# Mamba block: decay exponents by broadcast rows and a relu on ScalarE in place of matmuls with masked row constants

## The chip, the cores and the metric

The kernel runs on one core of a Trainium2 chip. The metric is the device time of one execution in microseconds (us); lower is better. TensorE is PE here, VectorE is DVE, ScalarE is ACT, GpSimd is POOL, and the queue of SyncE, which issues the DMAs, is SP.

## The reference

A block on 1024 tokens of width 512: a layer norm, then x plus a Mamba-2 mixer plus a small mixture of LoRA experts. The mixer is what matters. It has 128 heads of 64 channels, 8 groups of a 128-wide state, and chunks of 128 tokens:

```python
A_cum = jnp.cumsum(A_dt, axis=-1)                      # per head, inside a chunk
L = jnp.exp(_segsum(A_dt))                             # exp(A_cum[l]-A_cum[s]) for s<=l, else 0
Y_diag = jnp.einsum('bzlhn,bzshn,bhzls,bzshp->bzlhp', Cc, Bc, L, xch)
decay_states = jnp.exp(A_cum[..., -1:] - A_cum)
states = jnp.einsum('bzlhn,bhzl,bzlhp->bzhpn', Bc, decay_states, xch)
...
Y_off = jnp.einsum('bzlhn,bzhpn,bhzl->bzlhp', Cc, prev, jnp.exp(A_cum))
Y = (Y_diag + Y_off).reshape(b, s, H, P) + hs * D[None, None, :, None]
g = y * jax.nn.silu(gate)                              # then a group norm and out_proj
```

## The kernel before

The heads are worked in 16 stages s of 8 heads, and each stage in 8 chunks c of 128 tokens, so the main loop has 128 slots, m = 8s + c. Each engine runs its own list of instructions in order, and semaphores join them. Ahead of the loop stand the norm, the router, the LoRA part, the step sizes and their running sum A_cum (in the tile Q[1]).

In slot m, PE works through this, each item into one or two of the eight PSUM banks:
- T(m+1): four transposes of the 512 head channels of the next chunk (L285), and D(m+1): four bf16 matmuls (L292) that build, for all 8 heads, the 128x128 exponents A_cum[l] - A_cum[s], with about -3e38 where s > l. Their operands are constants (identity and mask, 64 rows) and rows of A_cum split into three bf16 parts, which three small DMAs per slot bring (`sp_rows`, tiles RM and RL). D takes banks 2 and 3.
- BG(m+1), in even stages alone: the transpose of B and the product G = B C of the chunk (L298, L299).
- A: input projection of a later stage, 12 matmuls for half a tile of 1024 tokens. Even stages have one half in each slot, odd stages 2, 1, 1, 2, 2, 1, 1, 2 halves, the last stage none.
- Off(m), St(m), Y(m): the old state's share, the new state, and the chunk's own share (32 small matmuls, L406, from EM and xch).
- O(m-1), 12 matmuls; GTr(m), transposes of the gated yb (L421); GT(m+1), 12 matmuls for the gate.

ACT in slot m (`act_front` first): the copy hsr of T(m+1) (L462); in even stages the copies BH, Gt and CH; the exponential over D(m+1) in PSUM (L476), ahead of which it loads its table; then tap (L446), SH, DH, the square sq of yb (L604), pl in even stages, gTh, OH at c=0, AH, the silu of a finished tile (L450), and the silu of GT(m+1) (L624).

DVE in slot m (`dve_front`, `dve_decay`): xch and dxh of the next chunk from T(m+1), with a wait for hsr; BL; then yb <- Off(m) (L807), the state S (L817), the product EM(m+1) = exp(D) * Gt (L659), yb <- Y(m) (L829), yb times the gate (L832), which releases sq on ACT and GTr(m) on PE; then the convolution of a tile (L635, three passes), gTl, and at c=0 OL. POOL makes dhs = hsr * D (L883), adds it to yb between L807 and L829 (L914), and makes the low parts SL, DL, CL, AL and GL.

A bank is given out again when the readers of its last user are through (`freed`). T's bank is free after xch and dxh, and in even stages St(m) takes the bank of T(m+1).

Of the kernel before, what the change touches and what calls it, by code (L numbers as in the profile page):

```python
# [6 lines left out]
def mamba_moe_block_kernel(nc, x, wa, wg, wo, wdt, cw, cbias, nw, dtb, alog, dvec, wbase, wrt, wla, wlb,  # L7
                           ident_c, rm_c, rl_c, ex_c, out):
# [3 lines left out]
    T, NS, NC, NB = 1024, 16, 8, 8  # L12
# [5 lines left out]
    par_d = nc.dram_tensor("par_d", [NS, 3, 8, NC, 128], bf16, kind="Internal").ap()  # L18
    sct_d = nc.dram_tensor("sct_d", [NC, 128, NS, 3, 8], f32, kind="Internal").ap()
# [33 lines left out]
    jobs += [("A", 3, (2, 3)), ("A", 4, (0, 1)), ("A", 5, (2, 3)), ("T", 0, (5,)), ("BG", 0, (6,)), ("D", 0, (2, 3)), ("GT", 0, (4,))]  # L53
# [43 lines left out]
    with ctx:  # L97
# [3 lines left out]
        def sem(name):  # L101
# [30 lines left out]
        dhs = sb("dhs", [128, 512])  # L132
# [10 lines left out]
        ident = sb("ident", [128, 128])  # L143
        Dbc = sb("Dbc", [128, 128])
# [53 lines left out]
        s_t, s_hsr, s_d, s_exp, s_bg, s_gb, s_bh, s_ch, s_bl, s_cl = (  # L198
            sem(n) for n in ("tp_", "hsr_", "dp", "exp", "bgp", "gb", "bh_", "ch_", "bl_", "cl_"))
# [15 lines left out]
            "T": lambda m: [(s_xch, m + 1)] + ([(s_dxh, n7(m))] if m % 8 != 7 else []),  # L215
            "D": lambda m: [(s_m, m + 1)], "BG": lambda m: [(s_bl, ngc(m))], "GT": lambda m: [(s_g, m + 1)],
# [33 lines left out]
        xs = [pl[0], pl[1], al[0], al[1], Sa, hsr, dxh, yb]  # L250
        sct_b = (xch[0], dhs, EM[1][:, 0:512], EM[1][:, 512:1024], S, pl[0], pl[1], al[0])
# [27 lines left out]
        def pe_front(m):  # L279
# [30 lines left out]
        def pe_program():  # L310
# [71 lines left out]
            for m in range(M + 1):  # L382
# [3 lines left out]
                if m < M:  # L386
# [16 lines left out]
                    for h in range(8):  # L403
                        at_ = (h % 2) * 512 + (h // 2) * 128
# [52 lines left out]
        def act_front(m):  # L457
            s, c = divmod(m, 8)
            se.wait_ge(s_t, m + 1)
            if m:  # L460
                se.wait_ge(s_dhs, m)
            se.activation(hsr[:, :], bank("T", m), ACT.Copy).then_inc(s_hsr, 1)  # L462
            if s % 2 == 0:
                o = bank("BG", m)
                se.wait_ge(s_bg, ngc(m))
                if s:
                    if c != 7:
                        se.wait_ge(s_stp, n7(m - 8))
                    if c:
                        se.wait_ge(s_off, n0(m - 8))  # L470
                    se.wait_ge(s_m, m - 7)
                se.activation(BH[:, c, :], o[:, 0:128], ACT.Copy).then_inc(s_bh, 1)
                se.activation(Gt[:, c, :], o[:, 128:256], ACT.Copy).then_inc(s_gb, 1)
                se.activation(CH[:, tok(c)], Cx[:, tok(c)], ACT.Copy).then_inc(s_ch, 1)
            se.wait_ge(s_d, m + 1)
            se.activation(pair("D", m), pair("D", m), ACT.Exp).then_inc(s_exp, 1)  # L476
# [15 lines left out]
        def act_program():  # L492
# [36 lines left out]
            se.wait_ge(s_rowsc, 4)  # L529
# [576 lines left out]
```

## Time and profile before

| | us |
|---|---|
| median of 3 runs | 1811.13 (1809.97 to 1813.1) |
| the profiled execution | 1813.75 |
| its span, first to last instruction | 1812.4 |
| PE busy | 1733.1 |
| ACT busy | 1279.0 |
| DVE busy | 1226.1 |
| POOL busy | 952.7 |
| mean granted TensorE clock | 0.992 of full |

The share of busy time is over the whole span. What sets the time of a slot is read from the engines' timelines: who waited for whom, and how long before it was needed each result was there. An "E slot" below is a slot of an even stage, an "O slot" one of an odd stage. The stretch from 776 to 988 us is one pair of stages (6 and 7), and E slots start again behind it. Start times of such slots are about 12.55 us apart for E slots.

### The profile page before, as it was taken

The page shows a single profiled execution, that of the slowest core. Times are in us where ns is not written, and L with a number is a line of the kernel's source. Part 1 is how long each engine was busy: PE and PEld are TensorE (multiplying, and loading weights), DVE is VectorE, ACT ScalarE, POOL GpSimd, SP SyncE. Part 2 cuts the span into 40 slices and gives each one's busy share as a digit, 9 for nine tenths or more (in the row PEclk, how much of TensorE's full clock was granted, in tenths as well). Part 3 has the DMA queues.
Part 4 walks back from the last instruction along what each step waited for, and adds up shares of the span by engine and source line. Part 5 has one row for each costly group of instructions (what it writes and reads, how often), then busy time and mean ns, then how long its engine had stood idle before and what let it go on. Part 6 is the DMA issues. An engine that isn't in the chain of part 4 may idle for free.

```text
span 1812.4 us, 32217 instructions
## 1 busy us (share of the span) xinstructions
PE 1733.1 (96%) x11748; PEld 1398.0 (77%) x11748; DVE 1226.1 (68%) x1594; ACT 1279.0 (71%) x1920; POOL 952.7 (53%) x973
## 2 busy tenths in 40 slices
PE   5989999999999999999999999999999999999988
PEld 3667878777887878778787777878787787877776
DVE  5846667766767658775677657776577656767666
ACT  4348776677767777777766777677776777667775
POOL 2125555545655555465555546555465555655475
PEclk8899999999999999999999999999999999999999
DMA  3141032220322113221332113231132212221022
GB/s 124 53 138 52 25 103 90 78 63 32 118 87 93 37 54 104 90 75 38 101 92 78 63 32 116 77 101 34 46 118 78 87 38 93 88 85 51 26 95 83
DMA packets 90699, 137.46 MB, mean 76 GB/s; under 512 B 38922, under 2 KB 40338, under 8 KB 86320
## 3 DMA queue, kind: packets, MB, share of 16 engines
q1 hardware_dynamic: 90544, 135.40, 23.7%
q8 instruction: 96, 1.57, 0.4%
q14 instruction: 59, 0.48, 0.1%
HBM read 97.34 MB, written 38.01 MB: 75 GB/s over the span
## 4 chain that ended last, share of the span: by engine, by line
PE 77%; DVE 10%; POOL 5%; issue 3%; ACT 2%; DMA 1%; SPq 1%; DVEq 0%; ACTq 0%; POOLq 0%
PE P L239 22%; PE P L241 20%; PE P L240 20%; PE P L406 5%; DVE hsX L635 4%; POOL GL L867 4%; PE P L285 3%; PE P L292 3%; PE P L421 2%; DMA EM<-in_rl_c 1%; DVE OL L853 1%; POOL yb L914 1%; ACT hsX L450 1%; DVE yb L829 1%; DVE yb L832 1%
## 5 line engine op out<-in xcount | busy, mean ns | idle before, releaser
L914 POOL TENSOR_TENSOR yb<-yb,dhs 128x512 f32<-128x512 f32 x112 | 143.8, 1284 | 634.3 <-DVE yb L807 634.3
L239 PE MATMUL P<-xh,AH 128*128 128x512 f32 x656 | 268.4, 409 | 1.1 <-POOL AL L862 1.1
L635 DVE SCALAR_TENSOR_TENSOR hsX<-P,cwt,hsX 128x1023 f32<-128x1023 f32 (+2 forms) x192 | 245.6, 1279 | 19.2 <-ACT hsX L446 14.6
L241 PE MATMUL P<-xh,AL 128*128 128x512 f32 x656 | 256.8, 391 | 0.0
L240 PE MATMUL P<-xl,AH 128*128 128x512 f32 x656 | 256.6, 391 | 0.0
L239 PE MATMUL P<-GH,xh 128*128 128x512 f32 x544 | 233.1, 429 | 8.1 <-POOL GL L867 7.3
L807 DVE TENSOR_TENSOR yb<-P,SC 128x512 f32<-128x512 f32 x112 | 77.3, 690 | 221.3 <-PE P L241 221.3
L645 DVE TENSOR_TENSOR xch<-P,SC 128x512 f32<-128x512 f32 x128 | 88.0, 687 | 190.0 <-ACT hsr L462 189.8
L241 PE MATMUL P<-GH,xl 128*128 128x512 f32 x544 | 216.0, 397 | 0.0
L239 PE MATMUL P<-OH,gTh 128*128 128x512 f32 x512 | 213.1, 416 | 2.5 <-issue 1.8
L240 PE MATMUL P<-GL,xh 128*128 128x512 f32 x544 | 214.6, 394 | 0.0
L604 ACT ACTIVATE sq<-yb 128x512 bf16<-128x512 f32 x128 | 80.9, 632 | 181.7 <-DVE yb L832 181.7
L241 PE MATMUL P<-OH,gTl 128*128 128x512 f32 x512 | 201.2, 393 | 0.0
L240 PE MATMUL P<-OL,gTh 128*128 128x512 f32 x512 | 200.5, 392 | 0.0
L873 POOL TENSOR_TENSOR SL<-S,SH 128x512 fp32r<-128x512 f32 x112 | 145.2, 1296 | 69.8 <-ACT SH L484 65.2
L406 PEld LDWEIGHTS P<-xch,EM 128*64 128x64 f32 x4096 | 129.9, 138 | 50.0 <-issue 42.8
L476 ACT ACT_TABLE_LOAD x128 | 164.2, 1283 | 2.2
L862 POOL TENSOR_TENSOR AL<-AR,AH 128x512 fp32r<-128x512 f32 x82 | 107.5, 1311 | 110.9 <-ACT AH L435 110.9
L659 DVE TENSOR_TENSOR EM<-P,Gt 128x1024 f32<-128x1024 f32 x128 | 155.5, 1215 | 3.5 <-ACT P L476 3.5
L406 PE MATMUL P<-xch,EM 128*64 128x64 f32 x4096 | 147.5, 225 | 4.5 <-DVE xch L645 3.3
L876 POOL TENSOR_TENSOR DL<-dxh,DH 128x512 fp32r<-128x512 f32 x112 | 145.1, 1296 | 9.6 <-ACT DH L490 9.6
L241 PEld LDWEIGHTS P<-xh,AL 128*128 128x128 f32 x656 | 123.7, 189 | 26.8
(188 smaller groups left out, 4031.9 us busy)
## 6 DMA issues: line engine op xcount, KB each, us to landing
AR<-in_wa SPq DMA_DIRECT2D x80, 256.0 KB, 2.9
TS<-in_wg SPq DMA_DIRECT2D x16, 1024.0 KB, 5.7
TS<-in_wo SPq DMA_DIRECT2D x16, 1024.0 KB, 5.4
part_d<-pl SPq DMA_DIRECT2D x64, 256.0 KB, 2.9
pl<-part_d SPq DMA_DIRECT2D x64, 256.0 KB, 2.7
al<-acc_d SPq DMA_DIRECT2D x64, 256.0 KB, 3.0
acc_d<-al SPq DMA_DIRECT2D x58, 256.0 KB, 3.0
RL<-par_d SPq DMA_DIRECT2D x256, 6.0 KB
```

What stands on the lines that cost most here:

```text
L239: te.matmul(o, ah_, bh_, start=(first and i == 0), stop=False)
L240: te.matmul(o, ah_, bl_, start=False, stop=False)
L241: r = te.matmul(o, al_, bh_, start=False, stop=(last and i == n - 1))
L406: r = te.matmul(o[f:f + 64, h * 64:(h + 1) * 64], EM[m % 2][:, at_ + f:at_ + f + 64], xch[m % 2][:, h * 64:(h + 1) * 64], start=True, stop ...
L476: se.activation(pair("D", m), pair("D", m), ACT.Exp).then_inc(s_exp, 1)
L635: ve.scalar_tensor_tensor(out=o[:, d:T], in0=raw[:, 0:T - d], scalar=cwt[:, n, 3 - d:4 - d], in1=o[:, d:T], op0=ALU.mult, op1=ALU.add).the ...
L645: ve.tensor_tensor(h8(xch[m % 2][:, :]), h8(o), bc(SC[s % 2][:, c, 0, :]), ALU.mult).then_inc(s_xch, 1)
L659: ve.tensor_tensor(EM[m % 2][:, :].rearrange("p (h l) -> p h l", h=8), pair("D", m).rearrange("p (h l) -> p h l", h=8), Gt[:, c, :].unsque ...
L862: pe_.tensor_tensor(AL[i % 2][:, :, :], AR[i % 2][:, :, :], as_f(AH[i % 2][:, :, :]), ALU.subtract).then_inc(ring_lo, 1)
L873: pe_.tensor_tensor(SL[:, :], S[:, :], as_f(SH[:, :]), ALU.subtract).then_inc(s_sl, 1)
L876: pe_.tensor_tensor(DL[:, :], dxh[:, :], as_f(DH[:, :]), ALU.subtract).then_inc(s_dl, 1)
L914: pe_.tensor_tensor(yb[:, :], yb[:, :], dhs[:, :], ALU.add).then_inc(s_tp, 1)
```

## The change

1. D(m) is no longer made by PE. A_cum goes to DRAM in f32 (`acr_d`), and one DMA per slot broadcasts the 8 rows of 128 values to all 128 partitions (tile AB, 512 KB written). ACT then makes the exponents in banks 2 and 3, head by head, with eight relus of 128x128: relu(A_cum[s] - A_cum[l]), where A_cum[s] is a per-partition bias from a fourth row group in SC. One exponential with scale -1 follows. Entries with s > l are 1 instead of 0.
2. G is masked once with a triangle by DVE when it leaves PSUM; ACT's copy Gt is gone.
3. hsr is gone. DVE makes dhs = T * D itself from PSUM (two buffers), behind dxh. POOL's product is gone. T's bank is free after dhs.
4. Ahead of the loop, the two loads of row constants, four casts of them and the split of A_cum into bf16 parts (five DVE operations, three stores) are gone; there are eight stores of A_cum, one more constant load, and SC is a third larger.

```diff
@@ pe_front
-            banks_free("D", m)
-            te.wait_ge(rows_in[m % 2], 48 * (m // 2 + 1))
-            v = pair("D", m).rearrange("p (q h l) -> p q h l", q=2, h=4)
-            for q in range(2):
-                for f in range(2):
-                    r = te.matmul(v[:, q, :, f * 64:(f + 1) * 64], RL[m % 2][0:79, q, f, :],
-                                  RM[m % 2][0:79, q::2, f * 64:(f + 1) * 64], start=True, stop=True)
-            r.then_inc(s_d, 1)
@@ act_front
-            se.activation(hsr[:, :], bank("T", m), ACT.Copy).then_inc(s_hsr, 1)
...
-                se.activation(Gt[:, c, :], o[:, 128:256], ACT.Copy).then_inc(s_gb, 1)
...
-            se.wait_ge(s_d, m + 1)
-            se.activation(pair("D", m), pair("D", m), ACT.Exp).then_inc(s_exp, 1)
+            for h in range(8):
+                r = se.activation(E[:, h, :], AB[m % 2][:, h, :], ACT.Relu, bias=SC[s % 2][:, c, 3, h:h + 1], scale=-1.0)
+            r.then_inc(s_gap, 1)
+            se.wait_ge(s_gap, m + 1)
+            se.activation(E[:, :, :], E[:, :, :], ACT.Exp, scale=-1.0).then_inc(s_exp, 1)
@@ dve_front
-            ve.wait_ge(s_hsr, m + 1)
+            ve.wait_ge(s_t, m + 1)
...
+            if m > 1:
+                ve.wait_ge(s_tp, n0(m - 2))
+                ve.wait_ge(s_t2, m - 1)
+            ve.tensor_tensor(h8(dhs[m % 2][:, :]), h8(o), bc(Dbc[:, 8 * s:8 * s + 8]), ALU.mult).then_inc(s_dhs, 1)
...
+                ve.tensor_tensor(Gt[:, c, :], o[:, 128:256], tri[:, :], ALU.mult).then_inc(s_gb, 1)
@@ pool_front
-            pe_.tensor_tensor(h8(dhs[:, :]), h8(hsr[:, :]), bc(Dbc[:, 8 * s:8 * s + 8]), ALU.mult).then_inc(s_dhs, 1)
@@ sp_rows
-                sp.wait_ge(s_d, m - 1)
-            sp.dma_start(RM[r][64:67, :, :], par_d[s, :, :, c, :]).then_inc(rows_in[r], 16)
-            for f in range(2):
-                sp.dma_start(RL[r][67:79, :, f, :],
-                             par_d[s, :, :, c, :].rearrange("i (h q) l -> (i h) q l", q=2)).then_inc(rows_in[r], 16)
+                sp.wait_ge(s_gap, m - 1)
+            sp.dma_start(AB[m % 2][:, :, :], acr_d[s, c:c + 1].broadcast_to([128, 8, 128])).then_inc(rows_in[m % 2], 16)
@@ dve_program, ahead of the loop
-            ve.wait_ge(rc_in, 32)
-            for r in range(2):
-                ve.tensor_copy(RM[r][0:79, :, :].rearrange("p h l -> p (h l)"), Qe[0:79, :]).then_inc(s_rowsc, 1)
-                ve.tensor_copy(RL[r][0:79, :, :, :].rearrange("p a b c -> p (a b c)"), EM[0][0:79, 0:512]).then_inc(s_rowsc, 1)
```

The order of ACT in an E slot of the first stage, from the silu of the gate to the square. Before (waits in brackets, by semaphore):

```order
L624 ACTIVATE P<-P 128x512 [waits gtp]
L462 ACTIVATE hsr<-P 128x512 [waits dhs_,tp_]
L472 ACTIVATE BH<-P 128x128 [waits bgp]
L473 ACTIVATE Gt<-P 128x128
L474 ACTIVATE CH<-Cx 128x128
L476 ACT_TABLE_LOAD
L476 ACTIVATE P<-P 128x1024 [waits dp]
L484 ACTIVATE SH<-S 128x512 [waits sl_,offp,st_]
L490 ACTIVATE DH<-dxh 128x512 [waits dl_,stp,dxh_]
L604 ACTIVATE sq,sqs<-yb 128x512 [waits sq_,g_]
```

The same place after the change:

```order
L613 ACTIVATE P<-P 128x512 [waits gtp]
L456 ACTIVATE BH<-P 128x128 [waits bgp]
L457 ACTIVATE CH<-Cx 128x128
L465 ACTIVATE P<-AB,SC 128x128 [waits m_,sc_in0,rows_in0]
L465 ACTIVATE P<-AB,SC 128x128 x7
L468 ACT_TABLE_LOAD
L468 ACTIVATE P<-P 128x1024 [waits gap]
L476 ACTIVATE SH<-S 128x512 [waits sl_,offp,st_]
L482 ACTIVATE DH<-dxh 128x512 [waits dl_,stp,dxh_]
L593 ACTIVATE sq,sqs<-yb 128x512 [waits sq_,g_]
```

Two copies have gone and eight relus stand ahead of the table load; the number of table loads is the same.

The order of DVE in an E slot, from gTl of one slot to yb of the next. Before:

```order
L848 TENSOR_TENSOR gTl<-P,gTh 128x512 [waits gth]
L645 TENSOR_TENSOR xch<-P,SC 128x512 [waits yp,sc_in0,hsr_]
L649 TENSOR_TENSOR dxh<-P,SC 128x512 [waits dl_]
L652 TENSOR_TENSOR BL<-P,BH 128x128 [waits gb]
L807 TENSOR_TENSOR yb<-P,SC 128x512 [waits sq_,gtr,offp]
L817 TENSOR_TENSOR S<-P,Sa 128x512 [waits sl_,sa_,stp]
L659 TENSOR_TENSOR EM<-P,Gt 128x1024 [waits exp,gb]
L829 TENSOR_TENSOR yb<-P,yb 128x512 [waits tpl,yp]
L832 TENSOR_TENSOR yb<-P,yb 128x512 [waits sg_,t2]
```

The same place after the change:

```order
L836 TENSOR_TENSOR gTl<-P,gTh 128x512 [waits gth]
L634 TENSOR_TENSOR xch<-P,SC 128x512 [waits yp,sc_in0,tp_]
L638 TENSOR_TENSOR dxh<-P,SC 128x512 [waits dl_]
L642 TENSOR_TENSOR dhs<-P,Dbc 128x512 [waits t2,tpl]
L648 TENSOR_TENSOR BL<-P,BH 128x128 [waits bh_]
L651 TENSOR_TENSOR Gt<-P,tri 128x128
L795 TENSOR_TENSOR yb<-P,SC 128x512 [waits sq_,gtr,offp]
L805 TENSOR_TENSOR S<-P,Sa 128x512 [waits sl_,sa_,stp]
L659 TENSOR_TENSOR EM<-P,Gt 128x1024 [waits yp,exp,gb]
L817 TENSOR_TENSOR yb<-P,yb 128x512 [waits tpl,yp]
L820 TENSOR_TENSOR yb<-P,yb 128x512 [waits sg_,t2]
```

dhs and Gt have joined the part between gTl and yb, and xch waits for the transposes themselves (tp_) and no longer for ACT's copy (hsr_).

## Rows read from the trace of the kernel before

**Rows 1.** The page, parts 1 and 4: busy time by engine; the chain that ended last.
```profile
PE 1733.1 (96%) x11748; PEld 1398.0 (77%) x11748; DVE 1226.1 (68%) x1594; ACT 1279.0 (71%) x1920; POOL 952.7 (53%) x973
...
PE 77%; DVE 10%; POOL 5%; issue 3%; ACT 2%; DMA 1%; SPq 1%; DVEq 0%; ACTq 0%; POOLq 0%
```

**Rows 2.** Timeline of PE in an E slot: start us, us, engine, line, out<-in.
```profile
803.22 0.60 PE L292 MATMUL P<-RM,RL 79*128 79x256 bf16 x4
803.66 0.27 PE L298 MATMUL P<-ident,Bx 128*128 128x128 f32 x1
...
824.67 0.60 PE L421 MATMUL P<-ident,yb 128*128 128x128 f32 x4
```

**Rows 3.** Groups by line and shape, ACT: busy us, mean ns, idle before.
```profile
L614 ACT ACTIVATE gTh<-P 128x512 fp32r<-128x512 f32 x128 | 76.2, 596 | 29.7 <-PE P L421 28.6
...
L618 ACT ACTIVATE OH<-TS,nwt 128x512 fp32r<-128x512 f32 x64 | 40.9, 715 | 1.8 <-DMA TS<-in_wo 1.8
...
L472 ACT ACTIVATE BH<-P 128x128 fp32r<-128x128 f32 x64 | 17.3, 270 | 5.0 <-PE P L299 2.1
```

**Rows 4.** Timeline of ACT: four scaled copies in a row.
```profile
891.35 2.56 ACT L618 ACTIVATE OH<-TS,nwt 128x512 fp32r<-128x512 f32 x4
```

**Rows 5.** Timeline of ACT: the exponentials of five slots, and one hsr copy.
```profile
806.15 1.01 ACT L476 ACTIVATE P<-P 128x1024 f32<-128x1024 f32 x1
...
819.19 1.01 ACT L476 ACTIVATE P<-P 128x1024 f32<-128x1024 f32 x1
...
883.34 0.60 ACT L462 ACTIVATE hsr<-P 128x512 f32<-128x512 f32 x1 [0.42 <-POOL dhs L883]
...
885.25 1.01 ACT L476 ACTIVATE P<-P 128x1024 f32<-128x1024 f32 x1
...
897.62 1.01 ACT L476 ACTIVATE P<-P 128x1024 f32<-128x1024 f32 x1
...
993.10 1.01 ACT L476 ACTIVATE P<-P 128x1024 f32<-128x1024 f32 x1
```

**Rows 6.** Timeline of DVE: the product EM of the same five slots.
```profile
808.90 1.21 DVE L659 TENSOR_TENSOR EM<-P,Gt 128x1024 f32<-128x1024 f32 x1
...
821.44 1.22 DVE L659 TENSOR_TENSOR EM<-P,Gt 128x1024 f32<-128x1024 f32 x1
...
886.96 1.22 DVE L659 TENSOR_TENSOR EM<-P,Gt 128x1024 f32<-128x1024 f32 x1
...
899.16 1.21 DVE L659 TENSOR_TENSOR EM<-P,Gt 128x1024 f32<-128x1024 f32 x1
...
994.63 1.21 DVE L659 TENSOR_TENSOR EM<-P,Gt 128x1024 f32<-128x1024 f32 x1
```

**Rows 7.** Timeline of ACT, an E slot: the square, with its wait for the gated y.
```profile
824.01 0.63 ACT L604 ACTIVATE sq<-yb 128x512 bf16<-128x512 f32 x1 [1.30 <-DVE yb L832]
```

**Rows 8.** Timeline of PE, slot c=1 of an E stage: its first matmul of St.
```profile
1007.36 0.47 PE L239 MATMUL P<-DH,BH 128*128 128x512 f32 x1 [1.51 <-DVE xch L645]
```

**Rows 9.** Timeline of ACT, last stage: an hsr copy and the exponential behind it.
```profile
1750.42 0.59 ACT L462 ACTIVATE hsr<-P 128x512 f32<-128x512 f32 x1
...
1752.32 1.01 ACT L476 ACTIVATE P<-P 128x1024 f32<-128x1024 f32 x1
```

**Rows 10.** Timeline of PE, last stage: GTr of two slots that follow each other.
```profile
1746.54 0.60 PE L421 MATMUL P<-ident,yb 128*128 128x128 f32 x4
...
1756.41 0.60 PE L421 MATMUL P<-ident,yb 128*128 128x128 f32 x4
```

**Rows 11.** The chain that ended last, before the loop: start us, us, what.
```profile
10.95 23.70 DMA EM<-in_rl_c
...
44.16 0.43 PE P L241
```

**Rows 12.** Timeline of DVE before the loop: the cast of the row constants, and its wait.
```profile
34.67 0.69 DVE L714 CAST RM<-hsX 79x1024 bf16<-79x1024 f32 x1 [8.91 <-DMA EM<-in_rl_c]
```

**Rows 13.** The page, part 6: DMA issues, KB each, median us to landing.
```profile
TS<-in_wg SPq DMA_DIRECT2D x16, 1024.0 KB, 5.7
```

More of the change, by code:

```diff
@@ L17, in mamba_moe_block_kernel @@
     part_d = nc.dram_tensor("part_d", [NC, 128, 512], f32, kind="Internal").ap()
[L18 to L19 removed]
+    acr_d = nc.dram_tensor("acr_d", [NS, NC, 8, 128], f32, kind="Internal").ap()
+    sct_d = nc.dram_tensor("sct_d", [NC, 128, NS, 4, 8], f32, kind="Internal").ap()
     eal_d = nc.dram_tensor("eal_d", [NS, 8, NC], f32, kind="Internal").ap()
@@ L121, in mamba_moe_block_kernel @@
         BL = sb("BL", [128, NC, 128], f32r)
-        SC = [sb(f"SC{i}", [128, NC, 3, 8]) for i in range(2)]
+        SC = [sb(f"SC{i}", [128, NC, 4, 8]) for i in range(2)]
         EA = [sb(f"EA{i}", [128, 8, NC]) for i in range(2)]
-        RM = [sb(f"RM{i}", [128, 8, 128], bf16) for i in range(2)]
-        RL = [sb(f"RL{i}", [128, 2, 2, 128], bf16) for i in range(2)]
+        AB = [sb(f"AB{i}", [128, 8, 128]) for i in range(2)]
         EM = [sb(f"EM{i}", [128, 1024]) for i in range(2)]
-        hsr = sb("hsr", [128, 512])
         xch = [sb(f"xch{i}", [128, 512]) for i in range(2)]
@@ L131, in mamba_moe_block_kernel @@
         DL = sb("DL", [128, 512], f32r)
-        dhs = sb("dhs", [128, 512])
+        dhs = [sb(f"dhs{i}", [128, 512]) for i in range(2)]
         yb = sb("yb", [128, 512])
@@ L248, in tok @@
             return slice(c * 128, (c + 1) * 128)
-        xs = [pl[0], pl[1], al[0], al[1], Sa, hsr, dxh, yb]
-        sct_b = (xch[0], dhs, EM[1][:, 0:512], EM[1][:, 512:1024], S, pl[0], pl[1], al[0])
+        xs = [pl[0], pl[1], al[0], al[1], Sa, dhs[0], dxh, yb]
+        sct_b = (xch[0], xch[1], EM[1][:, 0:512], EM[1][:, 512:1024], S, pl[0], pl[1], al[0])
         def tile_out(i):
@@ L458, in act_front @@
             s, c = divmod(m, 8)
[L459 to L476 removed]
+            if s % 2 == 0:
+                se.wait_ge(s_bg, ngc(m))
+                if s and c != 7:
+                    se.wait_ge(s_stp, n7(m - 8))
+                if s and c:
+                    se.wait_ge(s_off, n0(m - 8))
+                se.activation(BH[:, c, :], bank("BG", m)[:, 0:128], ACT.Copy).then_inc(s_bh, 1)
+                se.activation(CH[:, tok(c)], Cx[:, tok(c)], ACT.Copy).then_inc(s_ch, 1)
+            se.wait_ge(rows_in[m % 2], 16 * (m // 2 + 1))
+            se.wait_ge(sc_in[s % 2], 32 * (s // 2 + 1))
+            if m:
+                se.wait_ge(s_m, m)
+            else:
+                se.wait_ge(s_conv, 18)
+            for h in range(8):
[3 more added lines that the diff above has]
+            se.activation(E[:, :, :], E[:, :, :], ACT.Exp, scale=-1.0).then_inc(s_exp, 1)
         def act_state_hi(m):
@@ L828, in dve_program @@
                             ve.wait_ge(s_sq, m)
-                    ve.tensor_tensor(yb[:, :], bank("Y", m), (yb if c else dhs)[:, :], ALU.add).then_inc(s_t2, 1)
+                    ve.tensor_tensor(yb[:, :], bank("Y", m), (yb if c else dhs[m % 2])[:, :], ALU.add).then_inc(s_t2, 1)
                     ve.wait_ge(s_t2, m + 1)
```

96 lines of the change are left out of this document (37 added, 59 removed).

## The prediction, made before the changed kernel ran

> **What bounds the kernel now.** I read the page first: PE is busy for 1733 of 1812 us and holds 77% of the chain that ended last [rows 1]. So in nearly every slot PE issues matmuls back to back, and what it waits for lies elsewhere. I then read one E slot on PE: the next GTr stands 12.55 us behind the last, D's four matmuls hold PE from 803.22 until BG starts at 803.66, 0.44 us [rows 2]. Third, the timelines of ACT and DVE, for what is ready just in time. Two products matter. The exponential on ACT must be over before DVE makes EM(m+1) [rows 5, 6]. And DVE goes from EM through the two steps of yb to the gated y, which releases the square [rows 7] and GTr(m) on PE [rows 2]. In an E slot EM starts at 821.44, the square at 824.01 (2.57 us later), and GTr at 824.67, which is 0.66 us later still. I take 0.12 of that for the hand-over to PE, a choice, so that EM can be late by 0.54 us before PE stands still. Last, the stretch ahead of the loop: the chain holds 23.7 us for the load of the row constants [rows 11], and DVE stood 8.91 us for it [rows 12].
>
> **PE's side.** D goes in all 128 slots, 0.44 us each: 56 us, if nothing else becomes late. This is the ceiling of the loop's gain. POOL gives up dhs, and DVE takes it from PSUM as one more operation like its neighbours (about 0.6 us). In most slots it lies in the time in which DVE waited for hsr or for PE, and costs nothing; where that cover is absent it costs 0.6 us (slot c=1, below). The mask product for Gt on 128 columns lies there too.
>
> **ACT's side: eight relus.** No row shows a relu. The nearest is OH: SBUF source, one per-partition operand. It takes 715 ns for 512 columns [rows 3], and four take 2.56 us [rows 4], so one starts (2.56 - 0.715)/3 = 0.615 us after the other, an overlap of 0.10. From gTh (596 ns for 512) and BH (270 ns for 128) a column costs 326/384 = 0.85 ns [rows 3]. With 384 columns less, a relu takes 0.389 us, and the next starts after 0.289. Eight take 7 x 0.289 + 0.389 = 2.41 us. Bounds: below, a relu as cheap as BH with that overlap, 0.17, so 1.46 us for all (the output is PSUM, and the bias might be free); above, no overlap, 8 x 0.389 = 3.11 us. I take 2.41, from the row that has both the source and the operand. What goes is hsr (0.49 with its overlap, 0.59 where the table load follows it) and in E slots Gt (0.17). The exponential moves back by 1.75 us in E slots and 1.82 in O slots.
>
> **How late EM becomes.** The plan of PE shortens by 0.44 in every slot, so EM is wanted 0.44 earlier. EM is late by the move of the exponential, plus 0.44, less the time between the end of the exponential (start + 1.01) and EM now [rows 5, 6]; what exceeds 0.54 is a new wait of PE:
> - E, c=2 and 4 (EM 808.90): 1.75 + 0.44 - 1.74 = 0.45. No wait, the slot gains 0.44.
> - E, c=3 and 5 (821.44): 2.19 - 1.24 = 0.95, wait 0.41, gain 0.03. O, c=4 has the same make-up (no tap of its own behind a slot with a silu), and I give it the same.
> - E, c=6: late by 0.45, and here the convolution and silu behind yb release T of the next stage directly, with no slack. Gain 0.
> - O, c=0 (886.96): hsr had waited 0.42 for POOL's dhs [rows 5], which goes: 1.82 - 0.42 + 0.44 - 0.70 = 1.14, wait 0.60, a loss of 0.16.
> - O, c=1 (899.16): 1.82 + 0.44 - 0.53 = 1.73, wait 1.19, a loss of 0.75.
> - E, c=0 and 1 (994.63): the exponential ends 1.33 later (1.75 - 0.42), EM starts 0.81 later than now. Behind it stand yb, the convolution, gTl, OL, xch and dxh; St of c=1 waits for them in T's bank, 1.51 us already now [rows 8], and from now on for dhs too, 0.60. The pair of slots loses 0.81 + 0.60 = 1.41 instead of gaining.
> - E, c=7 gains 0.44, O, c=7 about 0.2 (the gate's high parts are late by the relus, and POOL's low parts behind them). The other O slots have two halves of A or a free ACT and gain 0.44 each, four of them.
>
> An even stage: +1.41 - 0.88 - 0.06 - 0.44 = +0.03 us. An odd one: +0.16 + 0.75 - 0.03 - 0.2 - 1.76 = -1.08. Seven pairs: -7.4 us.
>
> **The last stage** has no A to hide behind. There hsr starts at 1750.42 and GTr at 1756.41, slots are 9.87 apart [rows 9, 10]. With the relus the exponential ends at 1753.33 + 1.82 = 1755.15, EM starts at once, and GTr follows 2.57 + 0.12 later, at 1757.84: +1.43 us per slot. This holds for about seven slots: +10 us. With stage 14 as above the last pair costs 10 us.
>
> **Ahead of the loop.** DVE's wait of 8.91 us and four casts go [rows 12], at most 10.8 us; ACT's part of that chain then sets its pace, so I take 9. PE stood idle in that time, and the chain shows it afterwards at 0.43 us per matmul [rows 11], at half of the clock: twelve such in a row, some 2.5 us more than at full clock. Part of this should come back. The split into parts (five operations on DVE) was hidden behind PE. The wider SC copies cost below 1 us. I take -11, between -8 and -14.
>
> **The sum.** -7.4 + 10 - 11 = -8.4 us against the span of 1812.4, and against the profiled execution of 1813.75. The median of the runs is 2.6 us below that execution; I take the difference off the median, 1811.13, and forecast 1802 us. What a measurement can tell from no change here is about 0.2%, 3.6 us.
>
> **SP and the row load.** The broadcast brings 512 KB per slot in place of about 18. A load of 1 MB lands in 5.7 us [rows 13], so this one should in about 3 to 4, and it is issued two slots ahead; SP waits for the relus instead of D, up to 3 us later, ahead of the load of AR, which has a slot to spare. Cost nothing; without that cover it would be the 3 us once per slot. The removed loads of 79 rows were of another kind: 79 rows of 1536 f32 values, 474 KB, took 23.7 us with what stood ahead of them [rows 11]. The Trainium skill, DMA: Bandwidth & Descriptors, section Why a DMA increments its semaphore by 16 and not by 1, says that the number of DMA engines is the largest up to 16 that divides the slowest dimension of both sides: one engine for 79 rows, 16 for the 128 of the broadcast. By that rule the zero is right, and the row of the slow load agrees; if the broadcast were taken as 8 rows instead, it would get eight engines and land in about twice the time, still inside two slots.
>
> **The rivals.**
> - **Relus are cheap.** If the block takes 1.46 us, the list above with 0.95 us less gives -2.2 in an even and -3.3 in an odd stage, 5.5 for a pair, the last pair loses 1, and the time is 1811 - 38 - 11 + 1 = 1763. For: PSUM is the output. Against: OH's row has the same source and operand. Between 1.46 and 2.41 the time runs between 1763 and 1802. Chance 0.2.
> - **ACT becomes the bound.** If the relus don't overlap (3.11 us), seven slots of each pair lose 0.70 more and two E slots 0.61 each: 6.1 x 7 = 43, and 8 in the last pair: 1802 + 51 = 1853, slower. It decides from about 0.03 us more per relu: 63 slots x 0.21 us = 13 us take the time past 1814. For: in c=1 and in the last stage ACT has no free time at all. Chance 0.27. The Trainium skill, ScalarE: Activation LUTs, section Rules for kernel authors, would have a relu on VectorE and not on ScalarE; its section What ACT_TABLE_LOAD costs gives by an estimate 2.45 us for the block (280 ns + 0.833 ns per column, 93 ns overlap), and the sum would be 2 us longer. No run here shows a relu yet.
> - **The two sides cancel.** The gain ahead of the loop is paid back by the loop and the last stage, within 0.2% of 1811. Chance 0.13.
> - **My case**, 1788 to 1807, chance 0.4.
>
> **Chances and range.** Faster: my case and the cheap relus, 0.6; within 0.2%: 0.13; slower: 0.27. The range reaches from the cheap relus to half-way into the slow case: 1765 to 1840; my case alone has 1788 to 1807.
>
> **What would show it.** In the changed trace: a relu's mean near 0.39 us and eight of them in 2.4; D's 0.44 us gone from PE; new waits of PE ahead of GTr for yb L820, of 0.4 us in E c=3 and of about 1 us at c=1; slots of 11.3 us in the last stage; St of c=1 in even stages waiting over 2 us; the first loop transposes about 11 us earlier. The prediction is wrong if PE meets no new waits (time near 1750), or if taps and silus are late on ACT in slots with two halves.

## The result, and the profile after

| | before | after |
|---|---|---|
| median of 4 runs, us | 1812.12 (1809.97 to 1813.94) | 1834.35 (1832.9 to 1835.23) |
| span of the profiled run, us | 1812.4 | 1831.6 |

The ratio is 1.0122, with a 95% interval from 1.0105 to 1.014: the change made the kernel slower by 1.2%. 1802 us was predicted.

The page of the changed kernel, parts 1, 4, 5 (cut to the relus) and 6 (cut to the row load), to be held against [rows 1]:

```profile
PE 1699.5 (93%) x11244; PEld 1351.6 (74%) x11244; DVE 1311.6 (72%) x1777; ACT 1482.8 (81%) x2752; POOL 812.9 (44%) x845
...
PE 43%; DVE 22%; ACT 17%; issue 14%; POOL 3%; DVEq 0%; DMA 0%; ACTq 0%; SPq 0%; POOLq 0%
...
L465 ACT ACTIVATE P<-AB,SC 128x128 f32<-128x128 f32 x1024 | 307.4, 355 | 0.0
...
AB<-acr_d SPq DMA_DIRECT2D x128, 512.0 KB, 4.4
```

PE is busy for 34 us less, and its share of the chain that ended last has fallen from 77% to 43%: other engines now set many slots. DMA is not on the chain.

To see where, I took the start of each of the 128 squares (sq on ACT, one per slot) from the timelines of both kernels. Behind the last square stand 9.2 us in both kernels, so the differences add up to that of the span:

| part, us | before | after | difference | predicted |
|---|---|---|---|---|
| up to the first square | 146.01 | 133.47 | -12.5 | -11 |
| seven pairs of stages, 0 to 13 | 1489.1 | 1504.9 | +15.8 | -7.4 |
| stages 14 and 15, to the last square | 168.1 | 184.0 | +15.9 | +10 |
| sum | | | +19.2 | -8.4 |

The first of the seven pairs takes 213.2 us before and 213.1 after, so it loses nothing; the other six lose 2.5 to 2.7 us each. One of these, by slot (from the square of slot c-1 to that of slot c; + is slower, "pred." is what the list of the prediction gives):

| slot c | 0 | 1 | 2 | 3 | 4 | 5 | 6 | 7 |
|---|---|---|---|---|---|---|---|---|
| E, stage 8 | +0.27 | +2.06 | +0.67 | +0.51 | -0.46 | +0.50 | -0.47 | -0.45 |
| pred. | +1.41 for both | | -0.44 | -0.03 | -0.44 | -0.03 | 0 | -0.44 |
| O, stage 9 | +0.70 | +1.14 | -0.78 | -0.41 | +0.49 | -0.77 | -0.56 | +0.28 |
| pred. | +0.16 | +0.75 | -0.44 | -0.44 | -0.03 | -0.44 | -0.44 | -0.20 |

Timeline of ACT after the change, the E slot c=3 of stage 6 (start us, us, engine, line, out<-in, in brackets the idle time before it and what ended it):

```profile
806.94 0.63 ACT L593 ACTIVATE sq<-yb 128x512 bf16<-128x512 f32 x1 [0.52 <-DVE yb L820]
...
810.76 1.06 ACT L441 ACTIVATE hsX<-hsX 128x1024 f32<-128x1024 f32 x1 [0.31 <-DVE hsX L624]
...
812.59 2.40 ACT L465 ACTIVATE P<-AB,SC 128x128 f32<-128x128 f32 x8
815.01 1.28 ACT L468 ACT_TABLE_LOAD   x1
816.30 1.01 ACT L468 ACTIVATE P<-P 128x1024 f32<-128x1024 f32 x1
...
819.98 0.63 ACT L593 ACTIVATE sq<-yb 128x512 bf16<-128x512 f32 x1 [1.61 <-DVE yb L820]
```

DVE and PE in the same stretch:

```profile
806.82 3.90 DVE L624 SCALAR_TENSOR_TENSOR hsX<-P,cwt,hsX 128x1023 f32<-128x1023 f32 x3
...
817.40 1.22 DVE L659 TENSOR_TENSOR EM<-P,Gt 128x1024 f32<-128x1024 f32 x1 [1.33 <-ACT P L468]
```

```profile
807.10 0.60 PE L412 MATMUL P<-ident,yb 128*128 128x128 f32 x4
...
820.09 0.63 PE L412 MATMUL P<-ident,yb 128*128 128x128 f32 x4 [0.72 <-DVE yb L820]
```

The reader is to follow one loop: the gated y lets the convolution start (806.82), the silu waits 0.31 us for its end, the silu of the gate, two copies and the relus follow without a gap, then table load, exponential, EM (which waited 1.33 us), the next gated y, and GTr, for which PE waits 0.72 us. From square to square the loop takes 13.05 us (806.94 to 819.98). Its first square, that of slot c=2, began 0.16 us ahead of a GTr (807.10) for which PE did not wait. In the kernel before, the same square, in this row, began 0.65 us ahead of a GTr at 812.12:

```profile
811.47 0.63 ACT L604 ACTIVATE sq<-yb 128x512 bf16<-128x512 f32 x1 [1.30 <-DVE yb L832]
```

So the slot c=2 is late by 0.49 us at no cost of its own, and hands this on.

Slot c=1 of stage 8 on PE, and in the second fence on DVE:

```profile
1000.71 0.39 PE L240 MATMUL P<-SH,CL 128*128 128x512 f32 x1
1004.02 0.75 PE L238 MATMUL P<-DH,BH 128*128 128x512 f32 x1 [2.92 <-DVE dhs L642]
1004.57 0.63 PE L239 MATMUL P<-DL,BH 128*128 128x512 f32 x1
1005.00 0.63 PE L240 MATMUL P<-DH,BL 128*128 128x512 f32 x1
1005.56 1.98 PE L397 MATMUL P<-xch,EM 128*64 128x64 f32 x32
```

```profile
999.44 2.72 DVE L841 SCALAR_TENSOR_TENSOR OL<-TS,nwt,OH 128x512 fp32r<-128x512 f32 x4
1002.09 0.68 DVE L634 TENSOR_TENSOR xch<-P,SC 128x512 f32<-128x512 f32 x1
1002.69 0.67 DVE L638 TENSOR_TENSOR dxh<-P,SC 128x512 f32<-128x512 f32 x1
1003.29 0.67 DVE L642 TENSOR_TENSOR dhs<-P,Dbc 128x512 f32<-128x512 f32 x1
```

PE waits 2.92 us where it waited 1.51 in [rows 8], since St stands in T's bank behind OL, xch, dxh and now dhs. And what follows is slow: the step from matmul to matmul is 0.43 us (1004.57 to 1005.00), Y's 32 matmuls take 1.98 us. The windows of this stretch say why (us, busy us and count of PE, PEld, DVE, ACT, POOL, granted clock of PE, DMA share, GB/s):

```profile
1004.00:1007.40 3.40, 3.38 (x35) 2.58 (x35) 2.69 (x5) 1.89 (x3) 1.58 (x2) 0.51 0.96 399
```

The granted clock is 0.51, the lower of its two levels (1.2 GHz). In the kernel before, this slot had 1.00. The slots of the last stage are 11.43 us apart on PE, to be held against [rows 10] and against the 11.3 that was predicted:

```profile
1780.41 0.63 PE L412 MATMUL P<-ident,yb 128*128 128x128 f32 x4 [1.51 <-DVE yb L820]
...
1791.84 0.63 PE L412 MATMUL P<-ident,yb 128*128 128x128 f32 x4 [1.51 <-DVE yb L820]
```

Ahead of the loop, the first transposes start at 116.44, against 129.13 before.

### The profile page after: what moved, and what is told of

Read it like the earlier page. It is cut to its first block, busy times and chain, and to the rows that moved or that the text cites. A ratio compares the mean times of both kernels' runs of the same rounds, so it can differ in the third digit from the quotient of the medians.

```text
span 1831.6 us, 31670 instructions
## 1 busy us (share of the span) xinstructions
PE 1699.5 (93%) x11244; PEld 1351.6 (74%) x11244; DVE 1311.6 (72%) x1777; ACT 1482.8 (81%) x2752; POOL 812.9 (44%) x845
## 4 chain that ended last, share of the span: by engine, by line
PE 43%; DVE 22%; ACT 17%; issue 14%; POOL 3%; DVEq 0%; DMA 0%; ACTq 0%; SPq 0%; POOLq 0%
PE P L238 12%; PE P L240 11%; PE P L239 11%; DVE hsX L624 9%; ACT P L465 8%; DVE yb L820 4%; DVE yb L817 4%; PE P L397 3%; ACT P L468 3%; POOL GL L855 2%; PE P L284 2%; PE P L412 2%; DVE Bx L624 1%; DVE EM L659 1%; ACT P L613 1%
## 5 line engine op out<-in xcount | busy, mean ns | idle before, releaser
L465 ACT ACTIVATE P<-AB,SC 128x128 f32<-128x128 f32 x1024 | 307.4, 355 | 0.0
L397 PEld LDWEIGHTS P<-xch,EM 128*64 128x64 f32 x4096 | 135.0, 142 | 50.1 <-issue 44.6
L397 PE MATMUL P<-xch,EM 128*64 128x64 f32 x4096 | 152.9, 230 | 2.9 <-DVE dhs L642 2.9
```

Of the source, the lines that this page charges most:

```text
L397: r = te.matmul(o[f:f + 64, h * 64:(h + 1) * 64], EM[m % 2][:, at_ + f:at_ + f + 64], xch[m % 2][:, h * 64:(h + 1) * 64], start=True, stop ...
L465: r = se.activation(E[:, h, :], AB[m % 2][:, h, :], ACT.Relu, bias=SC[s % 2][:, c, 3, h:h + 1], scale=-1.0)
```

## The experiments

Times are medians of 4 to 9 runs; "before" stood at 1812.2 to 1813.1 us beside each group. "Pair" is the time of two stages in the middle: 212.64 us before, 215.3 after.

**one_relu.** How much of the loss is the block on ACT?

```diff
-            for h in range(8):
-                r = se.activation(E[:, h, :], AB[m % 2][:, h, :], ACT.Relu, bias=SC[s % 2][:, c, 3, h:h + 1], scale=-1.0)
-            r.then_inc(s_gap, 1)
+            se.activation(E[:, :, :], AB[m % 2][:, :, :], ACT.Relu, scale=-1.0).then_inc(s_gap, 1)
```

> The eight relus with a bias become one relu over all 1024 columns without a bias (so the bias is left out of the exponents; nothing else is left out). Its own time should be near the 1.01 us of the exponential, so that the block takes 1.4 us less than the 2.40 us measured in the changed kernel. Theory A (lateness: the relus stand on the chain from one slot's yb through convolution, silu, relus, exponential and EM to the next yb, and lateness is carried from slot to slot): the E pair of slots c=2 to 5 falls from 25.1 us to about 24.2 (PE's own time), the slots of the last stage from 11.41 to 10.0, and the whole to about 1768 us. Rival B (the cost is not ACT's: the row loads of 512 KB per slot or DVE's dhs hold the slots): the time stays above 1820 us, and the slots stay at 25.1 per pair. Rival C (the price of the block acts in every slot, ACT being the bound throughout): 128 times 1.4 us less, about 1655 us.

Measured: 1766.63 us, ratio 0.9738 (0.9722 to 0.9754). From its groups on ACT:

```profile
L464 ACT ACTIVATE P<-AB 128x1024 f32<-128x1024 f32 x128 | 130.0, 1016 | 0.0
```

With 1.4 us less on ACT, 68 us go. The E slots c=3 to 6 took 12.10 to 12.11 us each, the last stage's 10.03. Row loads and dhs were still there, so theory A (1768 us) is met to 1.4 us, and B and C fall. The same slots had taken 12.55 us before: what is left is the 0.44 us of D. It also puts a measured point beside the prediction's case of cheap relus (1763 us at 1.46 us for the block): with a block of only 1.02 us the time is 3 to 4 us above that.

**t_twice.** Is PE still the bound?

```diff
-            for t_ in range(4):
+            for t_ in (0, 1, 2, 3, 0, 1, 2, 3):
                 r = te.transpose(o[:, t_ * 128:(t_ + 1) * 128], hsX[s % 2][:, t_, tok(c)], ident[:, :])
```

> PE makes the four transposes of T twice, which gives PE back about the 0.44 us per slot that D's matmuls had taken; nothing is left out. Theory A: where the chain of ACT and DVE sets the slots (E c=1 to 5, the last stage) the extra work fits into PE's waits, the E pair stays near 25.1 us and the last stage at 11.41 us per slot; it costs 0.43 us in about six or seven slots of a pair of stages. Together some 15 to 25 us more than the changed kernel, about 1855 us. Rival (PE still sets nearly every slot, and the loss lies elsewhere): 128 times 0.43 us, about 1889 us.

Measured: 1866.47 us, 1.0283 (1.0266 to 1.03), 32 us above the changed kernel; 55 were possible, and I had expected 21. The last stage kept 11.4 us, and the E slots c=3 and 5 kept 13.05. But the other slots of these pairs went from 12.08 to 12.50: the pair has one slot that ACT's loop sets and one that goes through PE, where BG releases BH and the relus (T stands ahead of BG). More work on PE delays both alike; I had expected the second slot's extra to become slack for the first, and that was wrong.

**no_dhs.** Does DVE's extra operation cost?

```diff
-            if m > 1:
-                ve.wait_ge(s_tp, n0(m - 2))
-                ve.wait_ge(s_t2, m - 1)
-            ve.tensor_tensor(h8(dhs[m % 2][:, :]), h8(o), ...).then_inc(s_dhs, 1)
+            if m < 2:
+                ve.tensor_tensor(h8(dhs[m][:, :]), h8(o), bc(Dbc[:, 0:8]), ALU.mult).then_inc(s_dhs, 1)
```

> DVE makes dhs only in the first two slots; later slots add what those two left, so the D term of the other slots is left out, and T's bank is given free by xch and dxh. Theory A: dhs counts only where it stands between the end of OL and St of slot c=1 in even stages (PE waits 2.92 us there for dhs), 0.6 us for each of eight even stages, so about 5 us less than the changed kernel, 1829 us; the pair of E slots stays at 25.1 us. Rival (DVE's extra work counts in every slot): 128 times 0.6 us less, about 1757 us.

Measured: 1834.73 us, 1.0114 (1.0097 to 1.0131), the same as the changed kernel. The rival falls. Theory A's 0.6 us is there in most pairs (214.7 us in place of 215.3, and 213.2 in one), but in the profiled run the first square came 1.8 us later, and four slots of the last two stages took 13.0 us with a granted clock of 0.87, where the changed kernel had 11.4 to 11.9 at 1.00, and these took it back. Why the clock fell in just these was not tested.

**late_casts.** The part ahead of the loop by itself, in the kernel before: the row constants into EM[1] and xch[1], cast beside the third acc0.

```diff
-            sp.dma_start(Qe[0:79, :], rm_c).then_inc(rc_in, 16)
-            sp.dma_start(EM[0][0:79, 0:512], rl_c).then_inc(rc_in, 16)
+            sp.dma_start(EM[1][0:79, :], rm_c).then_inc(rc_in, 16)
+            sp.dma_start(xch[1][0:79, :], rl_c).then_inc(rc_in, 16)
```

> The kernel before with one change: the row constants are loaded into two other tiles and cast on DVE later, beside the third acc0, so that nothing waits for their load; nothing is left out. Theory A (the part ahead of the loop and the loop add up): the first transposes of the loop come 9 to 12 us earlier than at 129.13, the period of a pair of stages stays at 212.7 us, and the time is about 1801 us. Rival (the early start is given back before the loop's end): within 3 us of 1812 us.

Measured: 1810.10 us, 0.9978 (0.9967 to 0.9989); the first square 4.4 us earlier, not 9 to 12. Its chain, ahead of the loop:

```profile
13.82 21.43 DMA AR<-in_wa
```

Nobody waits for the row constants now, but the load of AR, next in SP's queue, takes 21.4 us, and ACT waits for it until 35.28. So the wait for the constants was not all that the slow load held up.

**rows128.** The kernel before, the two constants padded to 128 rows (`np.zeros((79, ...` becomes `np.zeros((128, ...`, and the loads take all rows).

> The kernel before with the two row constants padded from 79 to 128 rows with zeros, and loaded as such; more bytes, nothing else changed. In the kernel before, the load moves 25 to 27 GB/s for about 18 us, and with the casts moved away the next load of AR still took 21.4 us. Theory A (it is the 79 rows that are slow, one queue's share of the 16 engines): that stretch goes, the loads land in 3 to 6 us, the first square of the loop comes 10 to 12 us earlier than at 146.01, and the whole run is 8 to 12 us faster, about 1803 us. Rival (the bytes or the casts hold DVE): the first square within 2 us of 146.01, and the time within 3 us of 1812 us.

Measured: 1800.52 us, 0.9931 (0.9918 to 0.9945), the first square 10.0 us earlier. The DMA view from 0 to 60 us, GB/s in 40 slices, first of the kernel before, then of this one:

```profile
GB/s 0 212 346 304 358 347 354 275 354 322 33 27 25 27 27 25 27 111 265 26 25 26 26 15 0 0 0 119 67 0 0 0 0 0 5 51 124 0 0 0
```

```profile
GB/s 0 221 276 307 325 399 359 212 406 377 384 300 15 158 16 0 0 0 0 0 0 0 175 11 0 0 0 5 119 56 0 0 4 171 0 0 0 0 0 0
```

The stretches at 25 to 27 GB/s are gone, though more bytes were moved: it was the 79 rows. With them went DVE's wait of 8.91 us [rows 12], although its casts stayed:

```profile
26.70 0.69 DVE L714 CAST RM<-hsX 79x1024 bf16<-79x1024 f32 x1
```

By the Trainium skill, DMA: Bandwidth & Descriptors, section Why a DMA increments its semaphore by 16 and not by 1, 79 rows use one of 16 engines and 128 use all; the trace agrees, since 25 GB/s is one sixteenth of 400, near the highest of the view. The changed kernel has neither load, so the same 10 us should be in its 12.5; that was not measured apart.

**two_slots and odd_slots.** Is lateness carried? The changed kernel, with one relu in two slots of each even stage alone.

```diff
+            if s % 2 == 0 and c in (2, 4):        # odd_slots: (3, 5)
+                r = se.activation(E[:, :, :], AB[m % 2][:, :, :], ACT.Relu, scale=-1.0)
+            else:
                 (the eight relus)
```

> The changed kernel, but in even stages the block of slots c=2 and c=4 alone is one relu without bias, 1.4 us shorter (the bias is left out there). These are the exponentials without a silu ahead of them, before whose product PE did not wait: their lateness is 0.45 us by the prediction and costs nothing there by it. Theory A (their lateness is carried on: yb, convolution and silu of that slot start later, and the next exponential stands behind them): the pairs of E slots that follow fall from 25.1 us to about 24.7, as far as S on DVE allows; two pairs in eight stages, 6 us, about 1828 us. Rival (each slot on its own, as the prediction had it): the pair stays at 25.1 us and the time at 1834 us.

Measured: 1824.13 us, 1.0069 (1.0053 to 1.0084). In stage 8 the slots c=3 and 4 took 11.67 and 12.52 us, 24.2 for 25.1. But I had the slots exchanged: the block of c=4 runs ahead of the square of c=3, and in that slot the convolution's silu comes first. Each slot on its own would give this too, so it tells nothing apart.

> The changed kernel, but in even stages the block of slots c=3 and c=5 alone is one relu without bias, 1.4 us shorter (the bias is left out there). These are the exponentials without a silu ahead of them (the run before this one had shortened those with one). Ahead of their products' yb PE does not wait, so that by the prediction their lateness costs nothing. Theory A (it is carried on through yb, convolution and silu to the next exponential): the pairs of E slots that follow fall from 25.12 us to about 24.75 (EM can come 0.37 us earlier, then S on DVE holds it), two pairs in eight stages, 6 us, about 1828 us. Rival (each slot on its own): the pair stays at 25.1 us, the time at 1834 us.

Measured: 1822.64 us, 1.0046 (1.0031 to 1.0061). This is the test. The shortened block (that of c=5, which runs ahead of the square of c=4) is in a slot in which PE had not waited. That slot fell from 12.08 to 11.59 us, and the next, with silu and full block, kept 13.05: together 24.64 for 25.13. The 0.49 us is what the square of c=2 had been late. The rival falls. The whole fell by 11.7 us, where 6 were expected. The block of c=3 gave its part as well (c=1 and 2 together 29.2 in place of 29.6 us), and in stages 4 and 10 these two slots took 27.6 us: PE waited 2.93 us for dhs there as elsewhere, but its clock did not fall. The window behind that wait in stage 4:

```profile
571.70:573.70 2.00, 2.00 (x36) 1.52 (x36) 1.94 (x5) 1.14 (x2) 0.98 (x1) 1.00 0.95 397
```

**ol_late.** The wait at c=1.

```diff
+                    if c == 0 and m + 2 < M:
+                        dve_front(m + 2)
                     if c == 0:
                         for j in range(4):   (OL)
 ...
-                if m + 1 < M:
+                if m + 1 < M and c != 1:
                     dve_front(m + 1)
```

> The changed kernel; DVE makes the four OL of slot c=0 after xch, dxh and dhs of the next front instead of before them; nothing is left out. Theory A (dhs in T's bank, behind OL, is what St of c=1 waits 2.9 us for, and the clock falls after that wait): the wait goes, the granted clock stays at 1.00, and c=0 to c=2 of an even stage falls from 29.6 us to 27.5 or less, 12 to 20 us in all, about 1818 us. Rival (ACT's exponential or S is just as late there): 4 us or less, 1831 us.

Measured: 1820.89 us, 1.0039 (1.0025 to 1.0053), 13.5 us below the changed kernel. c=1 and 2 of stage 8 took 15.37 + 12.07 = 27.4 us in place of 29.6, at a clock of 1.00.

**filler.** Wait or clock? PE repeats Off's matmuls in the wait, and has more to do.

```diff
-                        mm3(bank("Off", m), [...]).then_inc(s_off, 1)
+                        for i in range(5 if c == 1 and s % 2 == 0 else 1):
+                            r = mm3(bank("Off", m), [...])
+                        r.then_inc(s_off, 1)
```

> The changed kernel, and in slot c=1 of even stages PE makes the three matmuls of Off five times over in the same bank, 12 matmuls of 0.23 us more, in the 2.92 us in which it waits for dhs. Nothing is left out; PE has 2.7 us more work in each of seven even stages. Theory A (after that wait PE's clock is granted at half for a time: St's three matmuls and Y's 32 took 3.4 us in place of 2.0): with the wait filled the granted clock stays at 1.00 and the slot from c=0 to c=1 is about 1.4 us shorter, 1824 us in all, faster with more work. Rival (the wait alone is the cost and the clock of no weight): the same time or longer, 1834 us or more.

Measured: 1824.23 us, 1.0065 (1.0052 to 1.0079). PE, at the same place:

```profile
1001.81 0.39 PE L240 MATMUL P<-SH,CL 128*128 128x512 f32 x1
1002.41 0.50 PE L238 MATMUL P<-DH,BH 128*128 128x512 f32 x1 [0.21 <-DVE dhs L644]
1002.75 0.40 PE L239 MATMUL P<-DL,BH 128*128 128x512 f32 x1
1002.98 0.40 PE L240 MATMUL P<-DH,BL 128*128 128x512 f32 x1
1003.31 1.15 PE L399 MATMUL P<-xch,EM 128*64 128x64 f32 x32
```

St and Y take 2.0 us in place of 3.4, and 12 more matmuls per even stage make the kernel 10 us faster. DVE's work is the same. So of the 13.5 us that ol_late gave back, about 10 are the clock's (each of the two times is good to about 3 us).

**pool_gap and pool_ol.** The exponents on POOL; in pool_ol with the order of ol_late as well.

```diff
+            for h in range(8):
+                r = pe_.tensor_scalar(AB[m % 2][:, h, :], AB[m % 2][:, h, :], SC[s % 2][:, c, 3, h:h + 1], 0.0,
+                                      ALU.subtract, ALU.min)
+            r.then_inc(s_gap, 1)
```

> The exponents are made on POOL instead of ACT: eight times (AB - bias) and then the minimum with 0, in place in the AB tile in SBUF, ahead of POOL's yb, where POOL waits 4.25 us in an E slot with AL and 6.62 us in one without; ACT makes the exponential from AB into the same PSUM pair. Nothing is left out. Nearest rows for the price: POOL's CL of 128 columns took 464 ns, its tensor_scalar on one column 191 ns, so 1.5 to 3.7 us for eight. Theory A (the relus' place on ACT's chain is the loss): E slots fall to PE's own 12.1 us as in the run with one relu, and the last stage to 9.3 to 9.6 us; the whole to about 1758 us, faster than both kernels. Rival (POOL takes the place of ACT: yb or SL come late): E slots over 12.5 us and a wait of DVE for POOL's yb, about 1800 us or more.

> As the kernel with the exponents on POOL, and DVE makes the four OL of slot c=0 after xch, dxh and dhs of the next front instead of before them; nothing is left out. Theory A (T's bank and with it St of c=1 wait for DVE's queue behind OL, which then lets PE's clock fall): PE's wait of about 2 to 3 us in c=1 goes and the granted clock stays at 1.00 there; the slot from c=0 to c=1 falls from about 15 us (14.9 to 15.1 with one relu) to about 13, for eight even stages and partly for the odd ones: 12 to 20 us less than the kernel with the exponents on POOL, about 1742 us. Rival (O then waits for OL instead): the same time as without the reordering.

Measured: 1880.1 us, 1.0372 (1.0358 to 1.0387), and 1870.36 us, 1.0317 (1.0303 to 1.0331). Groups on POOL, and the longest entry of the waits:

```profile
L857 POOL TENSOR_SCALAR AB<-AB,SC 128x128 f32<-128x128 f32 x1024 | 739.3, 742 | 0.0
```

```profile
ACT P L463 <- POOL AB L857: 349.6, 121, 4.9
```

One such operation of 128 columns takes 742 ns on average, where a difference of two tensors of that size takes 463 (CL). Eight take 5.8 us (739.3/128), outside my bounds of 1.5 to 3.7, and ACT waits for POOL in 121 of 128 slots.

**pool_sub, pool_sub_ol, early_sub, rows_first.** The subtraction alone on POOL, as one operation; one relu without bias on ACT. Then with the order of ol_late; then one slot earlier; then with AB's load ahead of pl's and al's in SP's queue.

```diff
+            pe_.tensor_tensor(AB[m % 2][:, :, :], AB[m % 2][:, :, :],
+                              SC[s % 2][:, c, 3, :].unsqueeze(2).broadcast_to([128, 8, 128]), ALU.subtract).then_inc(s_sub, 1)
 ...
             for m in range(M):
+                if m + 1 < M:             # early_sub, rows_first: m + 2
+                    pool_sub(m + 1)
```

> The exponents in two parts: POOL subtracts the bias from AB in one operation of 1024 columns with a broadcast operand, in place, ahead of its yb; ACT makes one relu of 1024 columns and the exponential, as in the run with one relu. Nothing is left out. Nearest row for POOL: Sa with a broadcast operand, 1.07 us for 512 columns, so 2.1 us, which fits into the 4.25 and 6.62 us that POOL waits ahead of yb (the eight operations of 742 ns each did not). Theory A (the loss is the block's 1.4 us on ACT): slots as in the run with one relu, 1767 us, faster than both kernels. Rival (POOL's part comes late as before): E pairs over 24.5 us and waits of ACT for POOL, 1790 us or more.

> As the kernel with the subtraction on POOL, and OL on DVE after xch, dxh and dhs of the next front. Nothing is left out. Theory A: PE's wait and the fall of its clock at c=1 of even stages go, 1 to 2 us for each of eight: about 1755 us. Rival: O waits for OL instead, the same time as without the reordering.

> As the kernel with the subtraction on POOL and OL behind the next front, but POOL subtracts for the slot after the next one, so one slot earlier, and so ahead of the four low parts of the gate (5.1 us) where a stage ends. Nothing is left out. There the slots had been 13.87 and 14.52 us long, against 11.57 and 12.33 with one relu and no subtraction. Theory A (the subtraction comes late behind POOL's queue in these slots and in the last stage, where a slot took 10.92 us against 10.03): these go back to about 11.6, 12.3 and 10.0, 2.3 + 2.2 us for each of seven pairs and 6 us in the last stage, about 1762 us. Rival (the load of AB is now what is waited for, since it is wanted a slot earlier): the slots of a stage's end stay over 13 us, 1790 us or more.

> As the kernel with the early subtraction, and SP issues the load of AB ahead of the loads of pl and al in each slot. In that kernel POOL waited 7.2 us for AB at the start of an odd stage: SP had stood until 864.31 for the store of part_d, which took 8.1 us beside the 1 MB of TS, and issued AB's load after it, at 865.16. Nothing is left out. Theory A (the first slot of odd stages took 14.4 to 14.8 us for that load, against 12.2 with one relu): this slot goes back to about 12.2 us, 2.4 us for each of seven or eight odd stages, about 1757 us. Rival (the load then delays pl and al, which DVE needs at the slot's end, or waits itself for the relu): 1772 us or more.

| | us | ratio | interval |
|---|---|---|---|
| pool_sub | 1824.97 | 1.0066 | 1.0052 to 1.0081 |
| pool_sub_ol | 1800.62 | 0.9928 | 0.9915 to 0.9942 |
| early_sub | 1774.97 | 0.9788 | 0.9774 to 0.9801 |
| rows_first | 1762.34 | 0.9718 | 0.9705 to 0.9732 |

For these four I had expected 1767, 1755, 1762 and 1757 us. In pool_sub the E slots c=3 to 6 fell to 12.1 us, as expected, but the time did not follow: where a stage ends the slots took 13.87 and 14.52 us. One slot earlier they took 11.56 and 12.33, and POOL met a new wait at the start of odd stages (POOL, then SP's queue, of early_sub):

```profile
870.75 1.90 POOL L861 TENSOR_TENSOR AB<-AB,SC 128x1024 f32<-128x1024 f32 x1 [7.23 <-DMA AB<-acr_d]
```

```profile
856.19 0.43 SPq L958 DMA_DIRECT2D part_d<-pl  x1
864.31 0.33 SPq L1012 DMA_DIRECT2D pl<-part_d  x1
864.68 0.43 SPq L1013 DMA_DIRECT2D al<-acc_d  x1
865.16 0.43 SPq L941 DMA_DIRECT2D AB<-acr_d  x1
```

SP stood from 856.6 to 864.3 for a store, with AB's load behind it. With that load first, the slot fell from 14.4 to 14.8 us to 12.7 to 13.3. The page of rows_first, parts 1 and 4:

```profile
PE 1680.4 (95%) x11244; PEld 1344.9 (76%) x11244; DVE 1335.3 (76%) x1777; ACT 1319.4 (75%) x1856; POOL 1053.9 (60%) x973
...
PE 70%; DVE 11%; issue 6%; ACT 6%; POOL 6%; DMA 1%; DVEq 0%; SPq 0%; ACTq 0%; POOLq 0%
```

It leaves out nothing of the reference, and is 50 us faster than the kernel before and 72 us faster than the changed one.

## Why the prediction was wrong

1834 us lies inside the range of 1765 to 1840, but that is luck: the range reached so far for a rival (relus without overlap, 1853 us) that did not come true. The forecast was a gain, with 0.6 for faster, and the loss came by other steps.

- **The price of the block: right.** 2.41 us predicted, 2.40 measured, 0.355 us for a relu and (2.40 - 0.355)/7 = 0.292 from one to the next (predicted 0.389 and 0.289). The rivals "relus are cheap" and "no overlap" fall; ACT did come to set slots, at the price at which I had said it would not.
- **D's 0.44 us on PE: right.** With one relu the E slots take 12.11 us for 12.55 before. Doubling T's transposes, 0.43 us, moved the slots that go through PE by 0.42.
- **E c=3, c=5 and O c=4: the failed step.** "E, c=3 and 5 (821.44): 2.19 - 1.24 = 0.95, wait 0.41, gain 0.03". The list took each slot with the slot before it on time. But "late by 0.45, no wait" of c=2 and 4 is still late: yb, convolution, silu and the next exponential follow, 0.49 us measured. 0.95 + 0.49 - 0.54 = 0.90 us, a loss of 0.46; measured +0.51 and +0.50 (of the wait, 0.72 us stood ahead of GTr). With +0.49 in O c=4 that is a loss of 1.5 us in three slots of a pair where a gain of 0.09 was predicted, 11 us in seven pairs. odd_slots shows the carrying in E slots; for O c=4 it is inferred from the size.
- **E c=0 and 1: place and wait right, price wrong.** PE waits 2.92 us for dhs, which is 1.51 + 0.81 + 0.60. But "the pair of slots loses 0.81 + 0.60 = 1.41" left out what the wait does to the clock. c=0 to 2 lost 3.0 us for 0.97 predicted, 12 us in the pairs (the first has no such wait). filler, which leaves DVE's lateness and takes the slow clock away, gave 10 us back; ol_late, which takes the wait away too, 13.5. The price is not a fixed one: in odd_slots the same wait twice left the clock at 1.00.
- **O c=0, 1, 7: too small.** Predicted +0.71 together, measured +2.12: 9 us in all, since the first pair does not have it. With one relu these slots went to 11.57, 12.20 and 13.09 us, so the block is the cause; by which path was not isolated.
- **The other slots gained more than the list has** (0.41 to 0.78 us each; E c=6, held at 0, gained 0.47): 1.3 us per pair, -9 us. Why O c=2 and c=5 gained 0.78 was not looked into.
- **Last stage: the slot right** (11.41, predicted 11.3), the count wrong: eight slots are late and not seven, by 11.8 us and not 10, and c=1 and 2 of stage 14 lose 4.1 us, more than in other even stages.
- **Ahead of the loop: right in size** (-12.5, predicted -11), with half of the cause. I put it on DVE's wait and casts. Taking these two away gave 4.4 us alone (late_casts), since the load of AR, behind the same slow load, was the next to be waited for. Making the load fast took both waits away, left the casts in place, and gave 10 (rows128). The part given back by the clock there was not singled out.
- **The row load: hidden, as said** (4.4 us; nothing in the changed kernel waits for it), until its user moved a slot earlier. **dhs on DVE: free apart from c=1**, as said.
- **The sum.** -8.4 became +19.2: pairs +23 (12 + 11 + 9 - 9), last pair +6, start -1.5.

## What to carry to other kernels

A list of slots, each with its own slack, is not enough where the late result feeds the next slot: follow one lateness through two slots before writing "no wait, no cost". A wait of PE is priced with the clock that follows it; here 2.9 us of waiting mostly cost 1.4 us more, and useless matmuls in its place paid. An operation that is moved to an idle engine inherits that engine's whole queue: ask for its place there, and for its load's place in SP's queue, before its price.

## What was not expected of the hardware

- A tensor_scalar on POOL with a per-partition operand and two operations took 742 ns for 128 columns; a tensor_tensor took 463 ns for 128 and 1.90 to 2.00 us for 1024 with a broadcast operand.
- After a wait of 2.92 us PE's clock was granted at 0.51 over the 3.4 us that followed; after 0.21 us of waiting at the same place it was 1.00. But in odd_slots it was 1.00 behind a wait of 2.93 us in stages 4 and 10, and 0.62 over 3.4 us in stage 6. With one relu the wait was 2.3 us, and the clock behind it 1.00 in stage 2 and 0.64 in stage 4. So the length of the wait alone does not tell; what else decides was not found.
- Behind loads of 79 rows at 25 GB/s a load of 256 KB took 21.4 us (late_casts), against 2.6 us for the median of its kind; with 128 rows the stretch at 25 GB/s was gone, and ACT did not wait for the load.
